# Half of the query and key projection, and all of v, moved into the first maximum pass of a transformer block kernel

## The reference, cut to what matters

```python
qkv = x @ w_qkv + b_qkv                      # x is the layer-normed input, (1, 4096, 256)
q, k, v = split into 16 heads of 16
scores = einsum('bqhd,bkhd->bhqk', q, k) * scale
attn = softmax(scores)
out = einsum('bhqk,bkhd->bqhd', attn, v)
```

## Time and profile before

| | us |
|---|---|
| median of 3 runs (lowest, highest) | 3106.18 (3104.97, 3108.98) |
| the profiled execution, its own time | 3108.23 |
| its span, first to last instruction | 3106.4 |
| PE busy | 3056.3 (98%) |
| DVE busy | 2822.5 (91%) |
| ACT busy | 2489.8 (80%) |
| POOL busy | 244.1 (8%) |

### The profile page before, as it was taken

One profiled execution on the slowest core, in us unless ns is written; L12 is line 12 of the kernel. 1 busy time (PEld: TensorE's weight loads), 2 busy tenths in 40 slices (PEclk: granted clock), 3 DMA queues, 4 the chain that ended last, 5 costly groups with the idle time before them and its releaser, 6 DMA issues.

```text
span 3106.4 us, 67882 instructions
## 1 busy us (share of the span) xinstructions
PE 3056.3 (98%) x26937; PEld 1337.5 (43%) x26937; DVE 2822.5 (91%) x3050; ACT 2489.8 (80%) x4539; POOL 244.1 (8%) x798
## 2 busy tenths in 40 slices
PE   8999999999999999999999999999999999999997
PEld 4544443443444343444444344344444344345765
DVE  5599999999999999999999999999999999957776
ACT  6278888888888888888888888888888888864444
POOL 2400000000000000000000000000000000001012
PEclk9799999999999999999999999999999999999999
DMA  7420101010110101010202010101001010000001
GB/s 261 63 42 1 39 5 35 8 29 15 22 22 15 28 11 33 5 39 1 42 1 42 1 39 5 32 12 25 18 18 25 15 28 16 16 1 1 1 8 48
DMA packets 27400, 83.03 MB, mean 27 GB/s; under 512 B 4657, under 2 KB 15649, under 8 KB 24034
## 3 DMA queue, kind: packets, MB, share of 16 engines
q1 hardware_dynamic: 26834, 77.84, 10.8%
q0 software_dynamic: 272, 1.05, 0.1%
HBM read 57.90 MB, written 20.97 MB: 25 GB/s over the span
## 4 chain that ended last, share of the span: by engine, by line
PE 92%; DVE 4%; ACT 2%; issue 1%; DMA 0%; POOL 0%; ACTq 0%; DVEq 0%; POOLq 0%
PE ps L1152 43%; PE ps L1161 37%; PE ps L1128 3%; PE ps L1087 2%; PE ps L1171 1%; PE ps L1349 1%; PE ps L1101 1%; PE ps L1179 1%; PE ps L1079 1%; PE ps L1294 1%; DVE partial L790 1%; DVE k_raw L861 1%; DVE q_raw L854 1%; ACT k_raw L633 1%; DVE q_raw L851 1%
## 5 line engine op out<-in xcount | busy, mean ns | idle before, releaser
L790 DVE TENSOR_REDUCE partial<-ps 128x1 f32<-128x1024 f32 x2048 | 2485.9, 1224 | 130.6 <-PE ps L1128 116.2
L568 ACT ACTIVATE work<-ps 128x512 f32<-128x512 f32 x4096 | 2207.7, 597 | 361.5 <-PE ps L1152 163.7
L1128 PE MATMUL ps<-k_stack,q_stack 48*128 48x512 f32 x4096 | 1533.1, 453 | 5.5 <-DVE partial L790 5.5
L1152 PE MATMUL ps<-q_stack,k_stack 64*128 64x512 f32 x4096 | 1510.1, 448 | 0.3 <-ACT work L568 0.3
L1161 PE MATMUL ps<-work,v_head 128*32 128x256 f32 x16384 | 1296.5, 391 | 0.0
L1152 PEld LDWEIGHTS ps<-q_stack,k_stack 64*128 64x128 f32 x4096 | 632.0, 184 | 805.5 <-ACT work L568 672.1
L1128 PEld LDWEIGHTS ps<-k_stack,q_stack 48*128 48x128 f32 x4096 | 634.3, 187 | 45.9 <-DVE partial L790 40.6
L1161 PEld LDWEIGHTS ps<-work,v_head 128*32 128x32 f32 x16384 | 329.2, 108 | 698.8 <-ACT work L568 579.5
L421 POOL CAST nm_parts<-negmax 128x4 bf16<-128x4 f32 x128 | 24.8, 194 | 2275.7 <-DVE negmax L797 2275.7
L1349 PE MATMUL ps<-k_raw,q_raw 128*128 128x256 f32 x512 | 123.1, 396 | 8.3 <-DVE attn L871 8.3
L560 ACT ACTIVATE q_stack<-ps 3x512 fp32r<-3x512 f32 x128 | 75.1, 587 | 52.5 <-PE ps L1179 49.5
(11 more groups left out here) (127 smaller groups left out, 1000.5 us busy)
## 6 DMA issues: line engine op xcount, KB each, us to landing
k_stack<-qk_parts SPq DMA_DIRECT2D x96, 256.0 KB, 4.1
q_stack<-qk_parts SPq DMA_DIRECT2D x96, 256.0 KB, 4.1
qk_parts<-qk_part SPq DMA_DIRECT2D x32, 512.0 KB, 2.8
x_sb<-L_attn_x SPq DMA_DIRECT2D x8, 512.0 KB, 11.0
out<-k_raw SPq DMA_DIRECT2D x4, 512.0 KB, 3.0
out<-v_head SPq DMA_DIRECT2D x3, 512.0 KB, 2.9
k_raw<-L_ffn_aux_values SPq DMA_DIRECT2D x1, 1024.0 KB
work<-L_attn_w_qkv POOLq DMA_DIRECT2D x1, 768.0 KB, 7.5
```

Source lines behind the costliest of these rows:

```text
L568: act.activation(probs[:, g % DEPTH, a, :], ps[:, bank, :], ACT.Exp, scale=SCALE).then_inc(exp_done, 1)
L790: dve.tensor_reduce(partial[:, k // 4, k % 4:k % 4 + 1], ps[:, 2 * slot:2 * slot + 2, :], AX.XY, ALU.max).then_inc(max_used, 1)
L1128: last = pe.matmul(ps[:, 2 * slot + e, :], q_stack[HALF:HALF + ROWS, b1, c * CH + (k // 4) * P:c * CH + (k // 4 + 1) * P], k_stack[HALF:HA ...
L1152: pe.matmul(ps[:, bank, :], k_stack[0:HALF, b, P * g:P * (g + 1)], q_stack[0:HALF, b, at:at + CH], start=True, stop=True).then_inc(s_ready, 1)
```

## The change

The jobs get a written-out order: first groups 0 and 2 of all chunks (16 jobs, `EARLY`), which hold heads 0 to 7, then groups 1 and 3 (16 jobs). Only the early ones are projected before the loads of head 0. The other 16 jobs and the 16 pieces of v form 16 blocks (one `project_qk` and one `project_v` each). Two blocks (`BLOCKS_FIRST`) come before PE waits for the first loads, 14 are laid between the 40 pieces of the maximum pass, after odd pieces, by `blocks_after`. Late jobs all use bank 4, v uses bank 7 and is read straight from `xnT` without ACT's copies. DVE's late splits come between its reductions, POOL's bias additions and `split_max` are interleaved by hand, and POOL's memsets of the stacks are cut into a half for buffer 1 (early) and one for buffer 0 (after all stores have landed). The hardware loops of this part are written out.

```diff
+    JOBS = [(c, g) for c in range(NC) for g in (0, 2)] + [(c, g) for c in range(NC) for g in (1, 3)]
+    EARLY = 2 * NC
+    FIRST_PIECES = AHEAD * 16 + LEAD
+    BLOCKS_FIRST = 2
+    def blocks_after(p):
+        return BLOCKS_FIRST + (p // 2 + 1) * (2 * NC - BLOCKS_FIRST) // (FIRST_PIECES // 2)
...
 # SP
+            for n in range(EARLY):
+                store_parts(n)
+            for r in range(4):
+                sp.wait_ge(parts_out[r], 16 * (EARLY // 4))
+            load_first((3, 4, 5), first_max_in)
+            load_first((0, 1, 2), first_score_in)
+            for n in range(EARLY, len(JOBS)):
+                store_parts(n)
...
 # POOL
+            pool.memset(k_stack[MROW:MROW + D, 1, :].bitcast(F32), 1.0).then_inc(rows_set, 1)
+            pool.memset(q_stack[MROW:MROW + D, 1, :].bitcast(F32), 0.0).then_inc(rows_set, 1)
...
+            for i in range(2 * NC):
+                bias_v(i)
+                if i == 8:
+                    split_max(0)
+                if i == 13:
+                    split_max(1)
+            pool.wait_ge(v_biased, 2 * NC)
+            copy_v(0, 1)
...
 # ACT
+            for c in range(NC):
+                evacuate_qk(2 * c)
+                if c + 1 < NC:
+                    move_xnT(c + 1)
+                evacuate_qk(2 * c + 1)
+            for i in range(2 * NC):
+                evacuate_qk(EARLY + i)
+                evacuate_v(i)
...
 # DVE
+            for c in range(NC):
+                if c + 1 < NC:
+                    dve.wait_ge(t_ready, c + 1)
+                    norm_chunk(c + 1)
+                split(2 * c)
+                if c + 2 < NC:
+                    dve.wait_ge(x_in[2], 16 * (NC - 2))
+                    x_stats(c + 2)
+                split(2 * c + 1)
...
+            for p in range(FIRST_PIECES):
+                row_max(0, range(p, p + 1), None, 0)
+                if p % 2 == 0:
+                    while done < (BLOCKS_FIRST if p == 0 else blocks_after(p - 1)):
+                        split(EARLY + done)
+                        done += 1
...
 # PE
+            for c in range(NC):
+                project_qk(2 * c)
+                if c + 1 < NC:
+                    pe.wait_ge(xn_ready, (c + 2) * TPC)
+                    transpose_chunk(xn, t_ready)
+                project_qk(2 * c + 1)
...
+            for i in range(BLOCKS_FIRST):
+                project_qk(EARLY + i)
+                project_v(i)
             pe.wait_ge(first_max_in, 16 * LOADS // 2)
+            done = BLOCKS_FIRST
+            for p in range(FIRST_PIECES):
                 for e in range(2):
+                    max_half(p % 16, e, p // 16, 1, p // 16, p % 2)
+                if p % 2:
+                    while done < blocks_after(p):
+                        project_qk(EARLY + done)
+                        project_v(done)
+                        done += 1
+                if p == AHEAD * 16 - 9:
+                    max_row(0, S_BANK[-2 % SRING])
             max_row(1, S_BANK[-1 % SRING])
             pe.wait_ge(vhead_ready, 1)
```

More of the change, by code:

```diff
@@ L289, in _, with store_parts @@
                 sp.dma_start(x_sb[:, TPC * c:TPC * (c + 1), :], x_t[:, TPC * c:TPC * (c + 1), :]).then_inc(x_in[min(c, 2)], 16)
[L291 to L295, removed]
+            def store_parts(n):
+                c, g = JOBS[n]
+                sp.wait_ge(split_done, n + 1)
+                dst = parts_dram[g // 2, :, (g % 2) * P:(g % 2 + 1) * P, CH * c:CH * (c + 1)]
+                sp.dma_start(dst.rearrange("r f t -> f r t"), qk_part[:, n % 4, :, :]).then_inc(parts_out[n % 4], 16)
             def load_first(slots, done):
@@ L365, in _ @@
                     pool.sem_inc(s, n)
-            for s in parts_out:
-                pool.sem_inc(s, 16)
             pool.sem_inc(primed, 1)
@@ L405, in copy_v, with bias_v @@
                 pool.tensor_copy(v_head[:, b, :, 0:D], v_rows[:, :, bass.ds(h * D, D)]).then_inc(vhead_ready, 1)
[L408 to L414, removed]
+            def bias_v(i):
+                pool.wait_ge(v_evac, i + 1)
+                pair = v_rows[:, 2 * i:2 * i + 2, :]
+                pool.tensor_tensor(pair, pair, bv, ALU.add).then_inc(v_biased, 1)
             def split_max(mi):
@@ L431, in split_max @@
                 pool.tensor_copy(nm_parts[:, :, 2], nm_rest[:, 1, :]).then_inc(nmparts_ready, 1)
-            with pool.Fori(0, AHEAD) as c:
-                split_max(c)
+            for i in range(2 * NC):
[6 more added lines that the diff above has]
+            copy_v(0, 1)
+            pool.wait_ge(vhead_ready, 1)
+            pool.wait_ge(split_done, len(JOBS))
+            for r in range(4):
+                pool.wait_ge(parts_out[r], 16 * (len(JOBS) // 4))
+            pool.memset(k_stack[MROW:MROW + D, 0, :].bitcast(F32), 1.0).then_inc(rows_set, 1)
+            pool.memset(q_stack[MROW:MROW + D, 0, :].bitcast(F32), 0.0).then_inc(rows_set, 1)
+            pool.wait_ge(rows_set, 4)
             def next_head(h, b):
@@ L513, in move_xnT, with evacuate_qk @@
                                ACT.Copy).then_inc(xnT_ready, 1)
[L515 to L520, removed]
+            def evacuate_qk(n):
+                c, g = JOBS[n]
+                r = n % 4
+                bank = 2 + r if n < EARLY else 4
+                act.wait_ge(qk_ready, n + 1)
+                if n >= 4:
+                    act.wait_ge(split_done, n - 3)
+                    act.wait_ge(parts_out[r], 16 * (n // 4))
+                act.activation(qk_f32[:, r, :], ps[:, bank, :], ACT.Identity, bias=bqk[:, g:g + 1]).then_inc(f_ready, 1)
+                act.activation(qk_part[:, r, 0, :].bitcast(F32R), ps[:, bank, :], ACT.Identity,
@@ L525, in _ @@
             move_xnT(0)
             act.wait_ge(w_in, 48)
[L527 to L551, removed]
@@ L931, in result @@
                 dve.tensor_scalar(o_nmean[:, b, lo:hi], o_mv[:, b, lo:hi, 0], -1.0, None, ALU.mult).then_inc(o_var, 1)
-            for c in range(AHEAD):
-                row_max(c, range(16), None, 0)
-            row_max(AHEAD, range(LEAD), None, 0)
+            done = 0
+            for p in range(FIRST_PIECES):
[4 more added lines that the diff above has]
+                        done += 1
+            while done < 2 * NC:
+                split(EARLY + done)
+                done += 1
             for it in range(ITS - 1):
```

95 lines of the change are left out of this document (29 added, 66 removed).

## The result

The changed kernel is slower: median 3137.91 us (four runs, 3135.69 to 3138.83) against 3107.40 for the kernel before on the same chip (four runs, 3104.97 to 3108.98), a ratio of 1.0099 [1.0087, 1.0111]. Forecast was 3116, 3104 to 3130; the direction was right, the size outside the range. The profiled execution took 3138.71, its span is 3136.9: 30.5 more than before, where +9.8 was forecast.

A forecast was written before the change was run, and what follows sets the result against it. PE, busy 98% of the span, bounded the kernel; the change touched only the lead before the first score. Terms -14.9, -2.4, -29.6, -50.6, +20.9, +85.5, +2.85, -2 gave +9.8 on 3108.2: 3118.0, median 3116, range 3104 to 3130.

The forecast's parts named there:

- Stage 1: Early projection with 16 jobs instead of 32: a chain of 6.2 a chunk, ending at 63.9 against 78.8, giving 14.9.
- Splits need not suffer: DVE's last early splits beside POOL's memsets of buffer 1: up to 2 x 3.5 possible, nothing taken.
- The loads: Wait before the maximum pass: queued loads follow each other, 15.65 from first issue to pass start at 84.8; PE idles 12.5.
- The pass: Maximum pass with 14 blocks laid between its pieces: 85.5 in all, ending at 170.3, at full clock after its start.
- Doubles: In the maximum pass, a pair without a block plus the next with one: 7.75 each, five make 38.8.
- single pair: In the maximum pass, a pair with its block where block follows block: 4.4 each, eight make 35.2.
- The end: Gap between the last block and the first score, waiting for the head's v: 2.85, where it was hidden before.
- I give back 2: First 9 us of the scores, at half clock before, might run at full clock: 2 gained, bounds 0 and 4.5.
- Behind the lead: Everything after the start of the scores: nothing changes, iterations of 41 us as before.
- Faster loads: Rival at the load wait: six loads land within 5.6 instead of 15.65, 9 to 10 us go, about 3106; chance 0.2.
- The pass hiding all waits: Rival in the maximum pass: DVE never late, clock full at once, pass 67.1, 18.4 less, 3098; chance 0.1.
- The clock falls more often: Rival in stage 1 and the pass: PE's clock falls, 1.7 each in the pass, total 3124 to 3132; chance 0.2.

The follow-up runs named there:

- e4: The changed kernel with four blocks instead of two before the wait for the first loads; 3140.7 us, ratio 1.0107 to the kernel before.
- e1: The changed kernel plus discarded 512-column matmuls in the maximum pass, where PE waited around pairs without a block; 3127.6 us, ratio 1.0064 to the kernel before.
- h3: g0 plus a discarded 256-column matmul behind each of the 40 pieces of the maximum pass; 3104.2 us, ratio 0.9989 to the kernel before.
- e3: The changed kernel with 28 single items (a job or a v piece) spread over all 20 pairs instead of 14 blocks; 3114.2 us, ratio 1.0024 to the kernel before.
- g2: The changed kernel with a third job in stage 1 chunks, 4 jobs and 7 v pieces in the load wait, 15 items in the pass; 3111.7 us.
- g3: The changed kernel with stage 1 kept, 4 late jobs and 6 v pieces in the load wait, 22 single items in the pass; 3108.9 us.
- h1: g2 with its late items cut into halves behind single pieces, discarded 256-column matmuls behind the other pieces, v in one bank; 3097.6 us.
- h2: g2 plus discarded 512-column matmuls behind pieces with no item near them, v in one bank in the pass; 3096.5 us, ratio 0.9967 to the kernel before.
- h4: The kernel before with v read from `xnT`, 12 v pieces before the pass, 4 in it, a discarded 256-column matmul behind each other piece; 3103.8 us.
- e2: e1 plus 14 discarded matmuls in the wait for the loads and 3 in the gap ahead of the scores; 3120.4 us, ratio 1.0041 to the kernel before.
- g0: The kernel before with v read straight from `xnT` without ACT's copies, all of it ahead of the pass; 3102.0 us, ratio 0.9991.

## Why the prediction was right in direction and short in size

**Stage 1: right, but for the clock.** Chain 6.2 forecast, 6.19 measured; last norm late beside a memset: +1.4 forecast, and it took 2.48 instead of 1.38 (+1.1). The one fall, from 25 to 31, was worth 2.6 (8.76 instead of 6.19 between two chunks), of which an earlier start took back 0.4. It stands behind an idle time of 3.32. The five chunks behind it have the same transposes, with waits of 1.29 to 2.76, and ran at full clock, so neither the transposes nor a wait longer than the 2.38 of before decide alone.

**"Splits need not suffer": right.** The splits beside POOL's memsets of the stacks took 0.69, as elsewhere. The Trainium skill ("SBUF — State Buffer", section "SBUF: two separate sides") says that a DVE instruction with two inputs from SBUF is held up only by a GpSimd one that reads SBUF; a memset reads nothing, and the 0.69 agrees.

**The loads: right.** 15.65 forecast from the first issue to the first piece, 15.9 measured; an idle time of 12.5, 12.27 measured. That the transfers come one behind the other was the dearest term of this stage, and e4 shows the same queue from the other side. What I had not said is that filling the wait needs buffers too.

**The pass: the structure right, the clock wrong and a term missing.** The start took 11.25 (11.1 forecast). The step that failed is the pass "with 14 blocks" costed at full clock behind its start. Doubles: 49.7 instead of 38.8. Four of five fell to half clock and cost 3.10, 1.69, 2.77 and 1.68 over the 8.09 of the one that did not, 9.2 together. I had this as a rival, at a chance of 0.2, because 1.37 without work had not lowered the clock before. That was reading one gap; in a double pair PE waits twice, 0.85 and 1.02, with one short piece between. The nearest row of before, 0.92 ahead of a piece at 112.80 with the clock at 0.50 from 116 on the earlier trace rows, pointed the same way. The rival's price of 1.7 a fall was also low: it was the loss of one stretch of v at 82, while here job and v behind it both ran slow at times. The Trainium skill ("TensorE: Matmul & The Clock Gate", section "A second HAM failure mode: psum-queue depth-cycling") reports of another kernel that frequent short idle times between groups of matmuls made the clock swing between its two levels; the waits of 0.85 and 1.02 ahead of the job of 3.78 agree with it, in four of five places, and I had not looked there.

The missing term is the handover. Two pieces between other work take 1.12 from start to start (105.77 to 106.89 in e1), one piece 0.66 (h3): 0.46 each and 0.2 for the visit. A job takes 1.82 instead of 1.72 and v 1.82 instead of 1.73. So a single pair is 4.77 and not 4.4, +2.9 over eight, and a double is 8.09 instead of 7.75, +1.7 over five. In the kernel before no row showed such an alternation, and I took the sum of parts that each ran alone. This is the term that was left out, not mis-sized.

**The end: right.** 2.77 for 2.85.

**"I give back 2": wrong, by 3.2.** From the first score to the first `move_o` it took 47.8 (188.82 to 236.60), before 46.6 (161.33 to 207.92), so even the lower bound of 0 was too good. I had asked whether the clock would be full behind the gap, and it was: 1.00 in the first 2.6 us. It then fell, with PE at work but for one wait of 0.28, and stayed at half for 10 us. All eight traces with 1.85 to 2.39 idle ahead of the first score show such a fall within their first steps (the changed kernel, e1, e3, e4, g2, g3, h1, h2: 45.6 to 50.5 to the first `move_o`). h3 and h4, where PE came from the pass into the scores without idle time, show none (44.1 and 44.0), and e2, with fillers in the gap, a short one (45.1). So this stretch is 3.7 longer in the changed kernel than in h3; why the fall comes after the idle time and not in it stays open.

**Behind the lead: nothing changes, right but for 1.8.** The iterations are 41.07 apart (41.08 before). The tail of 2.5 has no cause in the change that I could show. From the last `move_o` to the end it took 282.8 before and 285.4 in the changed kernel, and 279.3 to 283.7 in the twelve others, which run the same instructions there. g0 was 3.6 ahead at its first `move_o` (204.33) and 8.1 at its end (span 3098.3), with the same instructions between: so differences of some us there say nothing about an edit.

**The rivals.** Faster loads: excluded by 15.9. The pass hiding all waits: that is nearly h2 and not this kernel, where PE waits in every pair without a block. "The clock falls more often" had the mechanism, 3124 to 3132, and the time came 6 above it, because handovers (4.6), the start of the scores (3.2) and the tail (2.5) came on top, and no case of mine held two of these together. What stays open is why the same double pair fell four times and held once. Where the falls come is not fixed by the instructions: the same wait of 2.75 to 2.77 ahead of the last transposes of stage 1 was followed by a fall in e2, e3, e4 and g3 (6.40 to 7.01 for the three jobs behind it) and by none in the changed kernel and e1 (5.32).

## What to carry to other kernels

Laying one engine's idle stage over another's pays only if the engine with the clock stays loaded: cost the mixed stage at half clock as well, and see which pairs have nothing in them. Spread the moved work so that no visit is empty (e3: 24 us by order alone, 19 of them in the pass), add the price of each change between kinds of matmul, and count the buffers that stand behind a shared DMA queue before filling a wait. Where slack is left, a matmul whose result is thrown away can be cheaper than the wait, as long as it is about as long as the wait: 1.05 for 0.85 paid in e1, 0.63 for 0.40 did not in h3 (a ratio of 0.9989, g0 without fillers 0.9991).

## What was new about the hardware

- Added work made the kernel faster: 10 us by fillers in e1 (3137.9 to 3127.6, 6.0 of them in the pass), and 79.9 to 63.9 in the pass from g2 to h2.
- PE was busy for all of 10 us (192 to 202) at a mean granted clock of 0.52, and in g3 for 16.9 us at 0.50: full by the busy share and slow all the same. The same scores ran at 1.00 in h3 and h4.
- Changing between the pieces of 48 rows and matmuls of 128 rows costs about 0.2 a visit on the side of the pieces (0.66 for a piece instead of 0.46), and 0.1 each on the job and on v where the two come together, 0.2 on one that stands alone (1.92 in e3, 111.56 to 113.48).
- A store of 512 KB issued at 77.19 behind twelve loads on one queue had landed only by 101.5 in e4, 24 us later; the median of the stores of the kernel before is 2.8.
